# Last stage of a two-layer transformer kernel: the turns of a later pair's routings go behind the last two out_scale products

## The chip, the cores and the metric

The kernel runs on one core of a Trainium2 chip. The metric is the device time of one execution in microseconds (us), from the first to the last instruction with what lies around them. The kernel is one program of four stages that follow each other on the same core; its instructions are written out for each engine by hand, with semaphores between them. Engines are TensorE (PE in the rows), VectorE (DVE), ScalarE (ACT), GpSimd (POOL) and the DMA queue of SyncE (SP).

## The reference

Two layers, each a cross attention and a feed-forward part, on x of 16 batches x 128 positions x 1024. The change lies in the last part, a feed-forward layer with a sign matrix, whose input and output channels are scaled by a softmax routing over 8 experts:

```python
xf = x.reshape(-1, H)                                   # 2048 x 1024, after a layer norm
router_logits = xf @ gate_w.T                           # 8 experts
routing = jax.nn.softmax(router_logits.astype(jnp.float32), axis=1)
in_scale = routing @ in_channel_scale                   # 2048 x 1024
out_scale = routing @ out_channel_scale                 # 2048 x 1024
wb = ste_sign(weight)
out = xf * in_scale @ wb.T * out_scale + bias
x = x + jnp.tanh(g_ffn[1]) * out
```

## The kernel before

The function `sign_ffn_stage` works on pairs of batches; there are 8 pairs, p = 0 to 7, and batch b = 2p or 2p + 1. The loop over p is a software pipeline. In turn p TensorE computes the main products of pair p, the scale products of pair p + 1, and the turns, logits and turned routings of pair p + 2. VectorE also begins the norms of pair p + 3.

The names that the text uses, with the line of each in the profile:

- `main(p, u, part)` (L2411): output u of pair p, batch u // 2 and half u % 2 of the 1024 columns. Each output is two parts of 8 matmuls, 128 rows by 512 columns; the input is split in a rounded piece `xs_hi` and the rest `xs_lo`.
- `turn(b)` (L2362) transposes the normed batch, `logits(b)` (L2370) computes the router's logits, 16 rows by the profile for one batch's call (8 matmuls of 8 columns, two instructions each).
- `route_max`, `route_exp`, `route_share` make the softmax: VectorE's maximum (L2287), ScalarE's exponential (L2214), then on VectorE the reciprocal (L2293), the multiplication (L2296), two copies (L2300) and the rest of the split (L2302). The result is `rt3`, the routing in three pieces of 8, 24 columns in all.
- `turn_routing(b)` (L2378) transposes `rt3` on TensorE; it waits for `rt_hi` and `rt_lo`, which L2300 and L2302 raise. `routing_out(b)` (L2221) copies the result to `rT` on ScalarE.
- `in_scale(p, u)` (L2389) and `out_scale(p, u)` (L2399) multiply `rT` by the 24-row tables. All of them write two PSUM banks in turns, `p_s[0]` and `p_s[1]`. `scale(p, u)` (L2310) applies the in_scale on VectorE, `scale_out(p, u)` (L2226) copies the out_scale to `osc` on ScalarE. `out_scale(p, 2)` waits for `scale_out(p, 0)`, and `out_scale(p, 3)` for `scale_out(p, 1)`, since the bank is the same.
- `finish(p, u)` on VectorE multiplies the main product by `osc` (L2320) and adds it to x (L2323). `add_bias(b)` (L2178) runs on GpSimd, `round_hi` (L2232) on ScalarE and `lo` (L2172) on GpSimd split the scaled input for `main`, `rstd_of` (L2164, L2166) on GpSimd and `norm_apply` (L2280) on VectorE belong to the layer norm.

Each engine runs its own list in the order in which it is written; nothing reorders it, so an instruction that waits holds back all that stand behind it on its engine. VectorE's turn p ends with `finish(p, 2)`, `route_max(2p + 5)`, `route_share(2p + 4)`, `norm_apply(2p + 7)`, `route_share(2p + 5)`. The flags in the code are q (pair p + 1 exists), r (pair p + 2 exists) and z (pair p + 3 exists).

Of the kernel before, what the change touches and what calls it, by code (L numbers as in the profile page):

```python
# [2062 lines left out]
def sign_ffn_stage(nc, banks, x_in, gate, signW, bias, gate_wT, in_scale3, out_scale3, x_out):  # L2063
# [70 lines left out]
    def after(engine, done, count):  # L2134
        if count > 0:
            engine.wait_ge(done, count)

    def cols(b):
        return slice((b % 2) * SEQ, (b % 2 + 1) * SEQ)

    def half(h):
        return slice(h * BANK, (h + 1) * BANK)

    sp, pool, act, dve, pe = nc.sync, nc.gpsimd, nc.scalar, nc.vector, nc.tensor
    def load_x(b):
        sp.dma_start(x_sb[b % RING][:, :], x_in[b]).then_inc(x_land[b % RING], 16)
# [13 lines left out]
    def rstd_of(b):  # L2160
        i = b % 2
        pool.wait_ge(aggregated, b + 1)
        after(pool, xn_done, b - 1)
        G.tensor_tensor(rstd[i][:, :], mv[i][:, 1:2], eps[:, :], ALU.add).then_inc(eps_added, 1)  # L2164
        pool.wait_ge(eps_added, b + 1)
        G.tensor_tensor(rstd[i][:, :], rstd[i][:, :], half_neg[:, :], ALU.pow).then_inc(rstd_done, 1)  # L2166

    def lo(b):
        p = b // 2
        pool.wait_ge(hi_done, b + 1)  # L2170
        after(pool, main_done, 4 * (p - 2) + 4)
        G.tensor_tensor(xs_lo[p % 2][:, :, cols(b)], xs[:, :, cols(b)],  # L2172
                        xs_hi[p % 2][:, :, cols(b)].bitcast(F32), ALU.subtract).then_inc(lo_done, 1)

    def add_bias(b):
        pool.wait_ge(xn_done, b + 1)
        t = x_sb[b % RING][:, :]
        G.tensor_tensor(t, t, tgb[:, :], ALU.add).then_inc(xb_done, 1)  # L2178
# [214 lines left out]
    def out_scale(p, u):  # L2393
        b, h = 2 * p + u // 2, u % 2
        if u < 2:
            pe.wait_ge(xs_done, 4 * p + u + 3)
        else:
            pe.wait_ge(osc_out, 4 * p + u - 1)
        M(p_s[u % 2][:, :], rT[p % 2][:, cols(b)], ocs[:, half(h)], start=True, stop=True)\  # L2399
            .then_inc(out_scaled, 1)  # L2400

    def main(p, u, part):
        b, h = 2 * p + u // 2, u % 2
        if part == 0:
            pe.wait_ge(lo_done, b + 1)
            after(pe, y_done, 4 * p + u - 1)
        for k in range(4 * part, 4 * part + 4):
            if p == 0 and u == 0:
                pe.wait_ge(w_done, k + 1)
            for n, t in enumerate((xs_hi, xs_lo)):  # L2410
                mm = M(p_y[h][:, :], t[p % 2][:, k, cols(b)], w[:, k, half(h)],  # L2411
                       start=(k == 0 and n == 0), stop=(k == KT - 1 and n == 1))
        if part == 1:
            mm.then_inc(main_done, 1)
# [32 lines left out]
    def run():  # L2447
        stack = ExitStack()
        block = stack.enter_context(nc.Block())

        @block.gpsimd
        def _(_):
            for b in range(2, 6):
                rstd_of(b)
            pool.wait_ge(gate_done, 1)
            pool.wait_ge(bias_in, 16)
            G.tensor_scalar(tgb[:, :], tgb[:, :], tg[:, 0:1], None, ALU.mult).then_inc(bias_done, 1)  # L2457
            pool.wait_ge(bias_done, 1)
            add_bias(0)
            add_bias(1)  # L2460

            for p in range(NP):
                for i in range(2):
                    if p + 1 < NP:
                        lo(2 * p + 2 + i)
                    if p + 3 < NP:
                        rstd_of(2 * p + 6 + i)
                if p + 1 < NP:
                    add_bias(2 * p + 2)
                    add_bias(2 * p + 3)  # L2470

        @block.sync
        def _(_):
            load_x(3)
            sp.dma_start(tgb[:, :], bias).then_inc(bias_in, 16)
            for b in range(4, RING):
                load_x(b)
            for b in range(BATCH):
                sp.wait_ge(added, 2 * b + 2)
                sp.dma_start(x_out[b], x_sb[b % RING][:, :]).then_inc(x_store[b % RING], 16)  # L2480
                if b >= 1 and b - 1 + RING < BATCH:
                    sp.wait_ge(x_store[b - 1], 16)
                    load_x(b - 1 + RING)
            for i in range(RING):
                sp.wait_ge(x_store[i], 16 * len(range(i, BATCH, RING)))

        @block.scalar
        def _(_):
            for b in range(2, 4):
                turn_out(b)  # L2490
            for b in range(2, 4):
                route_exp(b)
            for b in range(2, 4):
                routing_out(b)

            for p in range(NP):
                if p + 1 < NP:
                    round_hi(2 * p + 2)
                    round_hi(2 * p + 3)
                if p + 2 < NP:  # L2500
                    turn_out(2 * p + 4)
                    turn_out(2 * p + 5)
                    route_exp(2 * p + 4)
                    route_exp(2 * p + 5)
                if p + 1 < NP:
                    scale_out(p + 1, 0)
                    scale_out(p + 1, 1)
                if p + 2 < NP:
                    routing_out(2 * p + 4)
                    routing_out(2 * p + 5)  # L2510
                if p + 1 < NP:
                    scale_out(p + 1, 2)
                    scale_out(p + 1, 3)

        @block.vector
        def _(_):
            for b in range(2, 4):
                norm(b)
            for b in range(2, 4):
                norm_apply(b)  # L2520
            for b in range(2, 4):
                route_max(b)
            for b in range(2, 4):
                route_share(b)
            for b in range(4, 6):
                norm(b)
            for b in range(4, 6):
                norm_apply(b)

            for p in range(NP):  # L2530
                q, r, z = p + 1 < NP, p + 2 < NP, p + 3 < NP
                if p >= 1:
                    finish(p - 1, 3)
                for u in range(2):
                    if q:
                        scale(p + 1, u)
                finish(p, 0)
                for u in range(2, 4):
                    if q:
                        scale(p + 1, u)  # L2540
                if z:
                    norm(2 * p + 6)
                finish(p, 1)
                if z:
                    norm_apply(2 * p + 6)
                    norm(2 * p + 7)
                if r:
                    route_max(2 * p + 4)
                finish(p, 2)
                if r:  # L2550
                    route_max(2 * p + 5)
                    route_share(2 * p + 4)
                if z:
                    norm_apply(2 * p + 7)
                if r:
                    route_share(2 * p + 5)
            finish(NP - 1, 3)

        @block.tensor
        def _(_):  # L2560
            turn(2)
            turn(3)
            logits(2)
            logits(3)
            turn_routing(2)
            turn_routing(3)

            for p in range(NP):
                q, r = p + 1 < NP, p + 2 < NP
                main(p, 0, 0)  # L2570
                for u in range(2):
                    if q:
                        in_scale(p + 1, u)
                main(p, 0, 1)
                for u in range(2, 4):
                    if q:
                        in_scale(p + 1, u)
                main(p, 1, 0)
                if r:
                    turn(2 * p + 4)  # L2580
                main(p, 1, 1)
                if r:
                    turn(2 * p + 5)
                main(p, 2, 0)
                if r:
                    logits(2 * p + 4)
                main(p, 2, 1)
                if r:
                    logits(2 * p + 5)
                main(p, 3, 0)  # L2590
                for u in range(2):
                    if q:
                        out_scale(p + 1, u)
                main(p, 3, 1)
                if r:
                    turn_routing(2 * p + 4)
                    turn_routing(2 * p + 5)
                for u in range(2, 4):
                    if q:
                        out_scale(p + 1, u)  # L2600

        stack.close()

# [80 lines left out]
```

## Time and profile before

| | |
|---|---|
| median of 3 runs | 3277.77 us (3274.28 to 3280.15) |
| profiled execution, its own time | 3282.62 us |
| profiled execution, span | 3280.8 us |
| mean granted TensorE clock | 0.966 |
| PE busy | 3080.3 us (94%) |
| DVE busy | 1950.1 us (59%) |
| ACT busy | 1229.2 us (37%) |
| POOL busy | 1964.6 us (60%) |

The own time is what the execution took by the device; the span is from its first to its last instruction in the trace. The loop that the change touches takes the last 190 us of the span or so. The granted clock is the share of TensorE's full clock of 2.4 GHz that it was given; 0.5 is 1.2 GHz. A matmul row's duration overlaps its neighbour's, since matmuls are pipelined, so the distance of two starts says more than a duration.

### The profile page before, as it was taken

To read this page: it belongs to the slowest core of one execution; us is meant where nothing else is said; L and a number is where in the kernel's file an instruction comes from. 1 tells how busy PE (TensorE), PEld (TensorE's weight loads), DVE (VectorE), ACT (ScalarE), POOL (GpSimd) and SP (SyncE) were. 2 spreads that over 40 slices of the span, in tenths; PEclk is the share of its full clock that TensorE was granted. 3 is DMA by queue.
4 is the path that set the end of the run, shared out by engine and by line. 5 is a ranking of instruction groups with operands and counts; after the bars stand their busy time and mean duration, and the time that the engine had idled before them with its cause. 6 is when DMAs were issued, how large, how long until landed. Compare 5 with 4: busy or idle time off the path is not lost. (4 is left out here: it accounts for less than half of the span.)

```text
span 3280.8 us, 41110 instructions
## 1 busy us (share of the span) xinstructions
PE 3080.3 (94%) x14547; PEld 2475.3 (75%) x14547; DVE 1950.1 (59%) x2479; ACT 1229.2 (37%) x1898; POOL 1964.6 (60%) x1372
## 2 busy tenths in 40 slices
PE   7999679999999996899999999989999899998799
PEld 6888558788787874677777777777777787777577
DVE  3332257777777753656565666656666566665575
ACT  3111155555555541333333333433333333343222
POOL 4232354454454443777787777777777777775343
PEclk9999889999999997899999999999999999999799
DMA  7343501101111113222233222332222332223211
GB/s 200 107 131 109 181 26 40 65 33 65 52 46 65 43 54 122 89 103 102 89 128 141 102 89 102 121 142 96 101 96 99 118 148 96 108 96 131 84 71 52
DMA packets 171261, 315.54 MB, mean 96 GB/s; under 512 B 10328, under 2 KB 86488, under 8 KB 171144
## 3 DMA queue, kind: packets, MB, share of 16 engines
q1 hardware_dynamic: 171144, 314.04, 27.2%
q8 instruction: 66, 1.08, 0.1%
q14 instruction: 51, 0.42, 0.0%
HBM read 246.90 MB, written 67.11 MB: 96 GB/s over the span
## 5 line engine op out<-in xcount | busy, mean ns | idle before, releaser
L1854 DVE RECIPROCAL g_rsum<-pair 128x512 f32<-128x512 f32 x128 | 429.8, 3358 | 112.9 <-PE pair L1924 109.0
L1892 PE MATMUL pair<-g_xn_hi,g_wq_hi 128*128 128x512 f32 x1024 | 403.6, 394 | 26.9 <-POOL g_wq_lo L1569 22.0
L1892 PE MATMUL pair<-g_xn_lo,g_wq_hi 128*128 128x512 f32 x1024 | 402.0, 393 | 0.0
L1892 PE MATMUL pair<-g_xn_hi,g_wq_lo 128*128 128x512 f32 x1024 | 401.6, 392 | 0.0
L1948 PE MATMUL pair<-g_wo_lo,g_at_hi 128*128 128x512 f32 x992 | 385.9, 389 | 0.0
L1948 PE MATMUL pair<-g_wo_hi,g_at_hi 128*128 128x512 f32 x992 | 385.9, 389 | 0.0
L1948 PE MATMUL pair<-g_wo_hi,g_at_lo 128*128 128x512 f32 x992 | 385.9, 389 | 0.0
L1840 DVE SCALAR_TENSOR_TENSOR g_res<-pair,g_tg,g_res 128x512 f32<-128x512 f32 x256 | 189.8, 748 | 208.9 <-PE pair L1948 207.2
L1569 POOL TENSOR_TENSOR g_wq_lo<-g_wq_raw,g_wq_hi 128x1024 fp32r<-128x1024 f32 x130 | 309.9, 2411 | 1.6 <-ACT g_wq_hi L1720 1.6
L1720 ACT ACTIVATE g_q_hi<-g_q_raw 128x512 fp32r<-128x512 f32 x128 | 81.0, 633 | 575.7 <-POOL g_q_raw L1650 575.7
L669 POOL TENSOR_TENSOR a_qs<-a_qs,a_qrec 128x512 f32<-128x512 f32 x128 | 133.8, 1047 | 202.5 <-DVE a_qrec L915 201.6
L1820 DVE TENSOR_TENSOR g_q_raw<-pair,t_cos_q 128x512 f32<-128x512 f32 x128 | 88.6, 692 | 274.2 <-POOL g_q_raw L1650 148.4
L1650 POOL TENSOR_TENSOR g_q_raw<-g_q_raw,g_rot_b 128x512 f32<-128x512 f32 x128 | 195.5, 1528 | 92.7 <-DVE g_rot_b L1822 92.7
L1892 PEld LDWEIGHTS pair<-g_xn_hi,g_wq_hi 128*128 128x128 f32 x1024 | 194.7, 190 | 71.1 <-POOL g_wq_lo L1569 25.0
L1892 PEld LDWEIGHTS pair<-g_xn_lo,g_wq_hi 128*128 128x128 f32 x1024 | 194.8, 190 | 40.5
L1892 PEld LDWEIGHTS pair<-g_xn_hi,g_wq_lo 128*128 128x128 f32 x1024 | 194.4, 190 | 40.9
L1569 POOL TENSOR_TENSOR g_q_lo<-g_q_raw,g_q_hi 128x512 fp32r<-128x512 f32 x128 | 165.1, 1290 | 95.1 <-ACT g_q_hi L1720 95.1
L1671 POOL TENSOR_TENSOR g_prob_raw<-g_prob_raw,t_keep 128x512 f32<-128x512 f32 x128 | 165.3, 1291 | 85.9 <-ACT g_prob_raw L1751 85.9
L1948 PEld LDWEIGHTS pair<-g_wo_hi,g_at_hi 128*128 128x128 f32 x992 | 186.2, 188 | 39.0
L1948 PEld LDWEIGHTS pair<-g_wo_lo,g_at_hi 128*128 128x128 f32 x992 | 186.2, 188 | 38.8
L1948 PEld LDWEIGHTS pair<-g_wo_hi,g_at_lo 128*128 128x128 f32 x992 | 186.2, 188 | 38.7
L1569 POOL TENSOR_TENSOR g_prob_lo<-g_prob_raw,g_prob_hi 128x512 fp32r<-128x512 f32 x128 | 166.1, 1297 | 47.5 <-ACT g_prob_hi L1720 47.5
(251 smaller groups left out, 7286.1 us busy)
## 6 DMA issues: line engine op xcount, KB each, us to landing
g_wq_raw<-in_L_Wq SPq DMA_DIRECT2D x64, 1024.0 KB, 7.3
g_wo_raw<-in_L_Wo SPq DMA_DIRECT2D x62, 1024.0 KB, 6.2
values_split<-c_v SPq DMA_DIRECT2D x64, 256.0 KB, 2.8
keys_split<-c_k SPq DMA_DIRECT2D x32, 512.0 KB, 2.7
g_k<-keys_split SPq DMA_DIRECT2D x32, 512.0 KB, 3.2
g_v<-values_split SPq DMA_DIRECT2D x32, 512.0 KB, 7.2
c_cx_raw<-in_ctxT SPq DMA_DIRECT2D x16, 512.0 KB, 7.5
a_x<-in_x SPq DMA_DIRECT2D x16, 512.0 KB, 4.4
```

The source lines that it names most:

```text
L669: TT(t, t, spread(qrec[r % 2][:, :], DH), ALU.mult).then_inc(qnorm, 1)
L1569: return engine.tensor_tensor(view(buf["lo"]), view(buf["raw"]), view(buf["hi"]).bitcast(F32), ALU.subtract)
L1650: nc.gpsimd.tensor_tensor(dst, dst, rot_b[:, :], ALU.add).then_inc(rot_done, 1)
L1671: nc.gpsimd.tensor_tensor(heads(e), heads(e), keep[:, :].rearrange("p (o t) -> p o t", o=1) .to_broadcast([P, G, SEQ]), ALU.mult).then_inc ...
L1720: return A(view(buf["hi"]), view(buf["raw"]), ACT.Copy)
L1820: V.tensor_tensor(by_batch(a), by_batch(src[:, :]), w(cos, 0, P), ALU.mult)
L1840: V.scalar_tensor_tensor(out=r, in0=p_y[u % 2][:, :], scalar=tg[:, 0:1], in1=r, op0=ALU.mult, op1=ALU.add).then_inc(y_added, 1)
L1854: V.reciprocal(rsum[:, :], p_sum[:, :]).then_inc(rsum_done, 1)
L1892: mm = M(bank[:, :], w[a][:, i, cols], x[b][:, i, :], start=(i == 0 and t == 0), stop=(i == KT - 1 and t == 2))
L1948: mm = M(p_y[u % 2][:, :], at[p][:, h, bcols(b)], w[r][:, h, half_ * BANK:(half_ + 1) * BANK], start=(h == 0 and t == 0), stop=(h == G - 1 ...
```

## The change

The two turns of the later pair's routings and the last two out_scale products change places at the end of a turn of TensorE's loop. Nothing else is changed: the other engines' lists are the same, and so are all waits.

```diff
@@ -2592,12 +2592,12 @@
                     if q:
                         out_scale(p + 1, u)
                 main(p, 3, 1)
+                for u in range(2, 4):
+                    if q:
+                        out_scale(p + 1, u)
                 if r:
                     turn_routing(2 * p + 4)
                     turn_routing(2 * p + 5)
-                for u in range(2, 4):
-                    if q:
-                        out_scale(p + 1, u)
```

On TensorE, at the end of the loop's turn p = 1 (the difference between before and after; L2411 main, L2399 out_scale, L2378 turn_routing), it looks like this:

```order
 L2411 MATMUL pair<-f_w,f_xs_hi_14045 128x512
 L2411 MATMUL pair<-f_w,f_xs_lo_14046 128x512
+L2399 MATMUL pair<-f_sc_14060,f_rT_14037 128x512 x2
 L2378 MATMUL pair<-f_ident,f_rt_0_14035 24x128
 L2378 MATMUL pair<-f_ident,f_rt_1_14036 24x128
-L2399 MATMUL pair<-f_sc_14060,f_rT_14037 128x512 x2
 L2411 MATMUL pair<-f_w,f_xs_hi_14042 128x512
 L2411 MATMUL pair<-f_w,f_xs_lo_14043 128x512
```

The two products now stand between the last main of pair 1 and the two turns; the first main of pair 2 follows directly behind the second turn. The same holds at six ends, p = 0 to 5.

On ScalarE, the same place, the list is the same before and after (L2232 round_hi, L2207 the turned input, L2214 the exponential, L2226 scale_out, L2221 routing_out):

```order
 L2232 ACTIVATE f_xs_hi_14042<-f_xs 128x8x128 x2
 L2207 ACTIVATE f_xnT_14040<-pair 128x4x128 x4
 L2214 ACTIVATE f_ex_14031,f_small_14029<-pair,f_small_14029 128x8
 L2214 ACTIVATE f_ex_14032,f_small_14030<-pair,f_small_14030 128x8
 L2226 ACTIVATE f_osc_14044<-pair,f_tg 128x512 x2
 L2221 ACTIVATE f_rT_14038<-pair 24x128 x2
 L2226 ACTIVATE f_osc_14044<-pair,f_tg 128x512 x2
```

Nothing moved here: the copies of the turned routings (L2221) stay ahead of the copies of the last two out_scale products.

## Rows read from the trace of the kernel before

**Rows 1.** The page's part 1: busy time by engine.

```profile
PE 3080.3 (94%) x14547; PEld 2475.3 (75%) x14547; DVE 1950.1 (59%) x2479; ACT 1229.2 (37%) x1898; POOL 1964.6 (60%) x1372
```

**Rows 2.** Waits of TensorE in the loop: total, times, longest.

```profile
PE pair L2378 <- DVE f_rt L2302: 4.9, 4, 1.2
PE pair L2362 <- ACT f_xnT L2207: 3.8, 1, 3.8
```

**Rows 3.** The chain that ended last, in the loop: start, us, what.

```profile
3108.54 2.05 PE pair L2411 x8
...
3113.95 2.04 PE pair L2411 x8
...
3133.02 0.27 PE pair L2378
3133.29 0.66 PE pair L2399 x2
3133.95 2.71 PE pair L2411 x8
...
3142.38 2.04 PE pair L2411 x8
...
3162.34 3.61 PE pair L2411 x8
...
3169.31 2.05 PE pair L2411 x8
...
3189.35 3.39 PE pair L2411 x8
...
3196.28 2.05 PE pair L2411 x8
...
3216.27 3.05 PE pair L2411 x8
...
3224.75 2.06 PE pair L2411 x8
```

**Rows 4.** Timeline of turn p = 1: start, us, engine, instruction, [idle before].

```profile
3121.14 0.39 PE L2411 MATMUL pair<-f_w,f_xs_lo 128*128 128x512 f32 x1
...
3123.07 0.49 PE L2411 MATMUL pair<-f_w,f_xs_hi 128*128 128x512 f32 x1
...
3125.21 0.69 DVE L2320 TENSOR_TENSOR f_y<-pair,f_osc 128x512 f32<-128x512 f32 x1 [0.24 <-PE pair L2411]
...
3125.80 5.17 POOL L2178 TENSOR_TENSOR f_x<-f_x,f_tgb 128x1024 f32<-128x1024 f32 x2
...
3128.91 2.10 DVE L2296 TENSOR_SCALAR f_rt<-f_ex,f_small 128x8 f32<-128x8 f32 x1
...
3129.27 1.26 ACT L2226 ACTIVATE f_osc<-pair,f_tg 128x512 f32<-128x512 f32 x2
...
3131.51 0.27 PE L2378 MATMUL pair<-f_ident,f_rt 128*24 128x128 f32 x1
...
3133.02 0.27 PE L2378 MATMUL pair<-f_ident,f_rt 128*24 128x128 f32 x1 [1.23 <-DVE f_rt L2302]
...
3133.75 1.27 ACT L2226 ACTIVATE f_osc<-pair,f_tg 128x512 f32<-128x512 f32 x2 [0.16 <-PE pair L2399]
```

**Rows 5.** Stretches: length, busy us of each engine, granted clock, DMA, GB/s.

```profile
3107.90:3133.00 25.10, 23.87 (x125) 18.51 (x126) 19.71 (x33) 7.91 (x17) 11.63 (x8) 1.00 0.24 85
3135.00:3138.40 3.40, 3.40 (x11) 2.25 (x10) 0.97 (x2) 0.02 (x1) 0.00 (x0) 0.51 0.89 305
3053.10:3056.50 3.40, 3.40 (x10) 2.62 (x9) 0.00 (x0) 3.08 (x4) 0.00 (x0) 0.51 0.00 0
```

**Rows 6.** TensorE's timeline ahead of the loop.

```profile
3050.22 0.72 PE L2399 MATMUL pair<-f_sc,f_rT 24*128 24x512 f32 x2
3051.55 1.07 PE L2399 MATMUL pair<-f_sc,f_rT 24*128 24x512 f32 x2 [0.60 <-ACT f_osc L2226]
3052.55 0.50 PE L1948 MATMUL pair<-g_wq_hi,g_at_hi 128*128 128x512 f32 x1
```

## The prediction

> **What bounds the kernel now.** I read the page first. TensorE is busy 94% of the span [rows 1], so whatever TensorE does not have to wait for is hidden. The change touches only the last stage, and there only the end of a pair's turn in the loop (b is a batch, a pair is two). I therefore asked the trace, in this order: who TensorE waits for in the loop, what the chain of waits looks like around each pair end, what the timeline shows at one such end, and what clock TensorE had.
>
> TensorE waits in the loop in two places only [rows 2]. One is a single 3.8 us at the first pair. The other is the one that the change touches: the turn of the routing (L2378) waits for VectorE's last piece of the split routing (L2302), 4 times, 4.9 us in all. The loop turns routings at six pair ends (p = 0 to 5); at p = 0 and p = 5 the routings are there in time. The four ends with a wait are p = 1 to 4, with the second turn at 3133.02 at p = 1 [rows 3] and 27 to 28 us apart from there on.
>
> The timeline of the end of p = 1 [rows 4] shows the order. The last product of main(1, 3, 1) ends at 3131.50, and the first turn goes at 3131.51, without a wait. The second can't start before 3133.02, since VectorE is late, 1.23 us of idle time. The two scale products (L2399, out_scale(2, 2) and (2, 3)) stand behind it, although nothing that they read or write is missing. Only after them, at 3133.95 by the chain, does the next pair's main begin [rows 3]. So the two products lie on the chain: 0.66 us at each of the four ends.
>
> Why is VectorE late? finish(1, 2) starts at 3125.21, 0.24 us after VectorE came free, so it waits for TensorE and not for its own work; GpSimd's two bias additions run from 3125.80 to 3130.97, and in that time VectorE's 128x8 multiplication (L2296) takes 2.10 us, to 3131.01 [rows 4]. All of that is tied to the in_scale products of the same pair: from their end, where main(p, 1, 0) begins, to the second turn it is 3133.02 - 3113.95 = 19.07 us [rows 3], and the next pairs repeat it. The Trainium skill, page "SBUF — State Buffer", section "SBUF: two separate sides", says that VectorE and GpSimd share a port pair which is locked for a whole instruction; the 2.10 us row agrees. The change moves nothing on either engine, so I leave the 19.07 us as it is.
>
> **The second thing at a pair end: the clock.** After each of these four waits the products slow down. At the end of p = 1 the chain goes from 3133.95 (start of main) to 3142.38 (start of main(2, 1, 0)), which is 8.43 us; the same work after the end without a wait took 3113.95 - 3108.54 = 5.41 us [rows 3]. The granted clock explains it: it is 1.00 (2.4 GHz) over all of 3107.90 to 3133.00, and 0.51, practically the low level of 1.2 GHz, in 3135.00 to 3138.40 [rows 5]. The other three ends give 3169.31 - 3162.34 = 6.97, 3196.28 - 3189.35 = 6.93 and 3224.75 - 3216.27 = 8.48 us [rows 3]. The excess over 5.41 is 3.02, 1.56, 1.52 and 3.07 us, together 9.17 us. This is three and a half times what the two products themselves cost.
>
> **The change, part by part.** No instruction is added or removed. On TensorE two products of 24x512 per pair end go ahead of two turns.
>
> 1. Out of the chain: 2 products, 0.66 us from the chain's row, at the 4 ends with a wait: **2.64 us**. They now run under the wait, from about 3131.50 to 3132.16. The first turn follows (0.27 us, to 3132.43), and the second still starts at 3133.02, since VectorE sets it. The wait left is 0.6 us. At p = 0 and 5 no wait exists, the order of four instructions changes and the sum doesn't: **0**.
>
> 2. A wait moved: out_scale(p + 1, 2) and (p + 1, 3) need ScalarE's copies of the products 0 and 1 out of the same two banks. At p = 1 these run 3129.27 to 3130.53 [rows 4]; TensorE comes at 3131.50. Margin 0.97 us, so **0**. Behind the two products the turns are queued, and behind them ScalarE's copies of the turned routings, the in_scale products and everything else. If the copies were late, all of it would be.
>
> 3. ScalarE's order is as it was: the two turned routings are copied before the scale copies 2 and 3. Before, those two copies ran from 3133.75 to 3135.02. Now their operands lie ready, and they can go behind the second routing copy: it ends some 0.57 us after the turn's start (0.30 to its start and 0.27), so 3133.6, and the pair of 1.27 us ends at 3134.9. The next in_scale products need both; at the full clock they come 2.05 us behind a main that starts at 3133.29, at 3135.3. Margin about 0.4 us for a copy that only the second of them needs: **0**. The other cover, main's own operands, is long there: GpSimd has no work between 3130.97 and the next pair.
>
> 4. The clock: up to **9.17 us**, and this is what has to be decided. The trace has no run of the new order, so I bound it from both sides by what TensorE did before the clock fell. What the four ends have in common is a break between full-size products (128x512 on 128 rows): from 3131.50 to 3133.95 at p = 1 [rows 3, 4], 2.45 us, in which TensorE has two turns, two small products and 1.2 us of nothing. Two earlier breaks of this stage are like it. From 3050.22 to 3052.55, 2.3 us with four 24-row products and 0.60 us idle [rows 6], and the clock was 0.51 in 3053.10 to 3056.50 [rows 5]. On the other side, the logits (16 matmuls of 8 columns) break the full-size products from 3121.14 + 0.39 = 3121.53 to 3123.07 [rows 4], 1.5 us, twice per pair, and the clock stays at 1.00 [rows 5]. With the change the break is 3131.50 to about 3133.25, 1.75 us. So the nearest row is the break of 1.5 us that the clock survived, and 2.3 us is the nearest that it did not. I take the value: no fall, 9.17 us. The lower bound is 0 (all falls stay); a fall that each time lasts as long as the longest one here gives 4 x 3.07 - 9.17 = 3.1 us loss, the bound below zero.
>
> The Trainium skill bears on this on both sides. "TensorE: Matmul & The Clock Gate", section "HAM oscillation — how this bites in real kernels", warns only of long pauses of TensorE; by that rule the clock should not have fallen here at all, with 1.23 us as the longest idle time [rows 4], and the trace contradicts it. The section "A second HAM failure mode: psum-queue depth-cycling" has short idle times between groups of products bring the clock down; by it the 0.6 us that is left could be enough, which is the first rival below.
>
> The sum against the profiled execution's own time, 3282.62 us: 3282.62 - 2.64 - 9.17 = 3270.8 us. That execution is 4.85 us above the median of the three runs (3277.77) and 2.5 above the slowest. How often the clock falls is something a run can differ in (1.5 or 3 us each), so part of the difference is probably a fall more than usual, and what isn't there can't be won. The whole sum off the median gives 3266.0; if all of the 4.85 us were falls, it gives 3270.8. I take the part near the middle: **3269**.
>
> **The rivals.**
> - The clock falls as before (0.6 us idle and two small products are still a disturbance; the break at 3050.22 had just 0.60 us idle). Then only step 1 is won: 3277.77 - 2.6 = 3275.1. For it: that break. Against it: its full-size gap was 2.3 us and had four small products. Chance 0.18.
> - The clock is saved at two of the four ends: 2.64 + 4.6 = 7.2 us off the own time, and 5 or so off the median: 3270 to 3275. Chance 0.12.
> - Nothing is won, as VectorE, given an earlier start, is late by as much again: finish(p, 2) had only 0.24 us of slack [rows 4]. But both it and main(p, 2, 1) are counted from the same in_scale products, so the slack doesn't shrink. 3277.8, chance 0.03.
> - Slower: the exponential of the later pair stands ahead of the scale copies 0 and 1 on ScalarE, and hangs on VectorE. If the copies end after 3131.50, TensorE stands in front of out_scale with both turns queued behind. Up to 3132.2 this costs nothing (3133.02 less 0.27 for a turn and about 0.5 for the products and their start). To be 6.6 us slower in all, with the falls kept, each of the four ends must lose 1.65 us beyond the 0.66 won, so the copies would have to end at about 3134.5, 4 us later than now. Price then 3284.4. Chance 0.04.
>
> **How the numbers follow.** The forecast (no fall at the four ends) has 0.63, its own range 3264 to 3273. A measurement of this kernel tells about 0.2%, 6.6 us, from no change, that is below 3271.2 for faster. The forecast lands there in about nine of ten cases (0.56), the half-saved case in one of three (0.04): faster 0.60. Same: the rest of the forecast 0.07, of the half-saved case 0.08, and the two cases at 3275 and 3278: 0.36. Slower 0.04. The range from 3263.5 to 3276 takes in the first rival and leaves out the last two and the tails.
>
> **What would show it.** In the changed kernel's trace the turns' wait falls from 4.9 to about 2.5 us in 4 places, the L2399 products at p = 1 to 4 directly follow main, and the full-size products resume 0.25 us after the second turn's start. The granted clock is 1.00 from about 3105 to the end, and turn to turn takes 24.8 us (28.39 - 0.66 - 3.02 = 24.7) instead of 26.9 to 28.4 (28.39 is the first period; the others follow from the sizes of their falls). I am wrong if the clock still shows 0.5 behind the second turns, if the second turn comes later than 19.1 us behind the in_scale products, or if TensorE shows a wait for ScalarE's f_osc.

## The result and the profile after

The changed kernel takes 3268.78 us in the median (3265.99 to 3275.14, 8 runs), the kernel before 3278.96 us (3273.85 to 3281.24, 8 runs): a ratio of 0.9973, 95% interval 0.9962 to 0.9984. It is faster by 0.27% by that ratio; the medians lie 10.2 us apart. The forecast was 3269 us.

Busy times by engine, the page's part 1 of the changed kernel (before: [rows 1]):

```profile
span 3267.3 us, 41110 instructions
...
PE 3066.2 (94%) x14547; PEld 2466.3 (75%) x14547; DVE 1948.1 (60%) x2479; ACT 1228.1 (38%) x1898; POOL 1964.4 (60%) x1372
```

The number of instructions is the same, yet TensorE's busy time fell by 14.1 us. Nothing was taken away from it: the same matmuls ran faster. Not all of this is the change's. In the first 3000 us of the span, where both kernels run the same code in the same order, TensorE was busy 2837.5 us in the trace of the kernel before and 2832.2 us in that of the changed one.

TensorE's waits in the loop (before: [rows 2]):

```profile
PE pair L2362 <- ACT f_xnT L2207: 3.8, 1, 3.8
PE pair L2378 <- DVE f_rt L2300: 2.6, 4, 0.7
```

The wait of the second turn is still there four times, at 0.65 us (once 0.69) instead of 1.24. The same place in the timeline, the end of the loop's turn p = 1 (before: [rows 4]):

```profile
3123.91 0.69 DVE L2320 TENSOR_TENSOR f_y<-pair,f_osc 128x512 f32<-128x512 f32 x1 [0.24 <-PE pair L2411]
...
3127.62 2.10 DVE L2296 TENSOR_SCALAR f_rt<-f_ex,f_small 128x8 f32<-128x8 f32 x1
...
3127.97 1.26 ACT L2226 ACTIVATE f_osc<-pair,f_tg 128x512 f32<-128x512 f32 x2
...
3130.13 0.73 PE L2399 MATMUL pair<-f_sc,f_rT 24*128 24x512 f32 x2
...
3130.79 0.28 PE L2378 MATMUL pair<-f_ident,f_rt 128*24 128x128 f32 x1
...
3131.73 0.27 PE L2378 MATMUL pair<-f_ident,f_rt 128*24 128x128 f32 x1 [0.65 <-DVE f_rt L2300]
...
3131.85 0.47 PE L2411 MATMUL pair<-f_w,f_xs_hi 128*128 128x512 f32 x1
...
3132.21 1.23 ACT L2226 ACTIVATE f_osc<-pair,f_tg 128x512 f32<-128x512 f32 x2
```

The products L2399 start at 3130.13 without a wait, 0.90 us after ScalarE's copies ended (3127.97 + 1.26 = 3129.23). Then comes the first turn, then the wait, the second turn at 3131.73, and main at 3131.85. VectorE's 2.10 us row and the 0.24 us in front of finish are what they were.

The chain behind two of the four ends (before: [rows 3]):

```profile
3112.66 2.05 PE pair L2411 x8
...
3131.73 0.27 PE pair L2378
3132.00 1.94 PE pair L2411 x8
...
3137.30 2.05 PE pair L2411 x8
...
3156.37 0.27 PE pair L2378
3156.64 2.08 PE pair L2411 x8
...
3162.09 2.05 PE pair L2411 x8
```

From the start of main(p, 1, 0) to the second turn it is 3131.73 - 3112.66 = 19.07 us, as before. From the start of main behind the second turn to the start of the next main(p, 1, 0) it is 3137.30 - 3132.00 = 5.30 us and 3162.09 - 3156.64 = 5.45 us, where it was 8.43 and 6.97.

Stretches from second turn to second turn, with the granted clock ahead of the two last numbers (before: [rows 5]):

```profile
3107.10:3131.70 24.60, 23.98 (x128) 18.65 (x128) 19.31 (x33) 7.88 (x17) 11.64 (x8) 1.00 0.25 86
3131.70:3156.40 24.70, 24.03 (x127) 18.73 (x127) 19.84 (x33) 7.71 (x16) 11.63 (x8) 1.00 0.25 86
3156.40:3181.20 24.80, 24.15 (x127) 18.69 (x127) 19.78 (x33) 7.71 (x16) 11.62 (x8) 1.00 0.25 87
3181.20:3205.80 24.60, 23.93 (x126) 18.61 (x127) 19.45 (x33) 7.72 (x16) 11.88 (x8) 1.00 0.11 43
3205.80:3229.60 23.80, 23.78 (x126) 18.64 (x127) 13.23 (x25) 7.45 (x15) 9.84 (x4) 1.00 0.11 45
```

The clock is 1.00 throughout. None of the four falls is left.

### The profile page after: what moved, and what is told of

Its sections match the earlier page's. It is cut to its first block and busy times, and to the rows that moved or that the text cites. A ratio compares the mean times of both kernels' runs of the same rounds, so it can differ in the third digit from the quotient of the medians.

```text
span 3267.3 us, 41110 instructions
## 1 busy us (share of the span) xinstructions
PE 3066.2 (94%) x14547; PEld 2466.3 (75%) x14547; DVE 1948.1 (60%) x2479; ACT 1228.1 (38%) x1898; POOL 1964.4 (60%) x1372
```

## The experiments

Two things had to be told apart: product time (the two products leave the chain, 0.66 us at each end) and the clock. And of the clock: what makes it fall, since the forecast took the break between full-size products for it. Each kernel was timed several times, but the two named again, of which there is one execution each. tail_small, tail_full, fill_before and one_product ran on one chip (kernel before 3279.76 us in the median of 24 runs), between_turns, the two share_first and bias_early together (3280.91, 13 runs), and the other four together (3280.39, 21 runs). The changed kernel's own partner took 3278.96 us, so two medians out of different groups can differ by up to 2 us for that alone. The ratios in brackets are each to the kernel before of the same group. Unless said otherwise the extra work of a kernel writes only an idle PSUM bank, and p means p = 1 to 4. A fall is a stretch behind an end in which the granted clock goes to its lower level of 1.2 GHz. The helpers `extra_small` and `extra_full` are not shown; they issue the matmuls that the comments name.

**Time put back, as small or as full products.**

```diff
                     turn_routing(2 * p + 5)
+                if 1 <= p <= 4:
+                    extra_small(p, 2)    # tail_small: rT x ocs, 24 rows, 128x512
+                    extra_full(p, 3)     # tail_full instead: xs_hi x w, 128 rows, 128x512
```

tail_small: 

> The changed kernel with two more 24-row products (128x512, into an idle bank; their result is used by nobody) behind the second turn at p = 1 to 4. It puts back what the change took out of the chain and leaves the order of the real work as changed. Theory (a long break between full-size products makes the clock fall): the break is 2.4 us again, the clock falls behind the second turns, and the time is that of the kernel before, 3279 us, within 4. Rival (only the 0.66 us of product time counts, the clock falls by chance): 2.6 us above the changed kernel, 3271.4.

tail_full: 

> The changed kernel with three more full-size matmuls (128x512 on 128 rows, 0.23 us each, into an idle bank, result unused) behind the second turn at p = 1 to 4. It lengthens the chain by as much as the two small products did, 0.69 us at each end, but the break between full-size products stays 1.75 us. Theory: no fall, 3268.8 + 2.8 = 3271.6 us. Rival (anything that delays the pair brings the falls back): 3279.

tail_small took 3273.64 us (ratio to before 0.9977, 0.9965 to 0.9988), tail_full 3270.53 (0.9972, 0.9961 to 0.9983). By the medians the full-size products cost close to their time and no more: 1.8 us over the changed kernel, 2.8 expected. The small ones cost 4.9 us, 2.6 of it product time. That is not the whole way back to 3279. The two intervals overlap almost wholly, so the times alone don't show that small products cost more than full-size ones. In tail_small's trace one of the four ends has a fall; stretches just behind the ends p = 1 and p = 4:

```profile
3136.40:3139.80 3.40, 3.40 (x16) 2.52 (x16) 1.23 (x3) 0.61 (x2) 0.00 (x0) 1.00 0.71 252
...
3212.30:3215.60 3.30, 3.30 (x9) 2.42 (x8) 0.50 (x1) 0.95 (x2) 0.00 (x0) 0.53 0.39 159
```

So my first theory did not hold as a rule. A break of 2.4 us with 0.65 us of idle time in it went with a fall at one end and with none at three.

**The wait filled, the order left as before.**

```diff
                 if r:
                     turn_routing(2 * p + 4)
+                    if 1 <= p <= 4:
+                        extra_full(p, 4)    # fill_before; small_filled: extra_small(p, 3)
                     turn_routing(2 * p + 5)
```

fill_before: 

> The kernel before, in its order, with four more full-size matmuls between the two turns at p = 1 to 4, under the wait of the second (0.92 us of 1.23; result unused). The real products stay where they were, on the chain. Theory: the break between full-size products ends at 1.1 us, the clock holds, and 9 of the 12 us are won without the change: 3270 to 3272 us. Rival (the order of the products itself does it): no gain, 3279.

small_filled: 

> The kernel before, in its order, with three more 24-row products (about 1 us; result unused) between the two turns at p = 1 to 4, under the wait of the second. The idle time goes from 1.24 to about 0.3 us, the break between full-size products stays 2.45 us. Theory A (the break decides): as the kernel before, 3279 to 3280. Theory B (idle time decides): as fill_before, 3272 to 3273.

fill_before took 3272.86 us (0.9976, 0.9966 to 0.9986). That is 6.9 us under the kernel before of its group: most of the gain comes with no product moved, by work that is thrown away. Its trace has a control in it. At p = 0 nothing was filled, and in this execution that end had a wait too. TensorE's timeline at p = 0, then at p = 1 (L2418 is the filling):

```profile
3103.51 0.27 PE L2378 MATMUL pair<-f_ident,f_rt 128*24 128x128 f32 x1 [1.24 <-DVE f_rt L2302]
...
3128.95 1.17 PE L2418 MATMUL pair<-f_w,f_xs_hi 128*128 128x512 f32 x4
3130.43 0.27 PE L2378 MATMUL pair<-f_ident,f_rt 128*24 128x128 f32 x1 [0.32 <-DVE f_rt L2300]
3130.64 0.73 PE L2399 MATMUL pair<-f_sc,f_rT 24*128 24x512 f32 x2
```

and the stretches behind p = 0, 1, 2, 3 and 4:

```profile
3104.80:3108.10 3.30, 3.30 (x10) 2.23 (x9) 0.00 (x0) 0.70 (x2) 0.00 (x0) 0.53 0.78 263
...
3130.90:3134.30 3.40, 3.40 (x15) 2.28 (x15) 1.18 (x3) 1.38 (x3) 0.00 (x0) 1.00 0.54 181
...
3156.30:3159.70 3.40, 3.40 (x15) 2.27 (x15) 1.22 (x3) 1.37 (x3) 0.00 (x0) 1.00 0.54 177
3181.70:3185.10 3.40, 3.40 (x16) 2.26 (x15) 1.19 (x3) 1.33 (x3) 0.00 (x0) 1.00 0.38 154
3207.00:3210.40 3.40, 3.40 (x15) 2.31 (x15) 1.22 (x3) 1.44 (x3) 0.00 (x0) 1.00 0.38 154
```

The unfilled end falls to 0.53, the four filled ones stay at 1.00.

small_filled took 3276.59 us (0.9992, 0.9983 to 1.0001), 3.8 us under the kernel before of its group by the medians, but the interval does not exclude that nothing was gained. The profiled execution took 3283.20 us, the second slowest of 11. Its trace has all four falls, although the idle time was only 0.33 to 0.35 us. Stretches behind the four ends:

```profile
3135.20:3138.50 3.30, 3.30 (x12) 2.14 (x10) 0.33 (x1) 0.44 (x1) 0.00 (x0) 0.56 0.71 245
3162.50:3165.80 3.30, 3.30 (x9) 2.36 (x9) 0.74 (x2) 1.35 (x3) 0.00 (x0) 0.56 0.51 178
3189.80:3193.10 3.30, 3.30 (x9) 2.24 (x8) 0.44 (x1) 1.18 (x2) 0.00 (x0) 0.56 0.39 159
3217.10:3220.40 3.30, 3.30 (x10) 2.18 (x10) 0.12 (x1) 0.86 (x2) 0.00 (x0) 0.56 0.39 159
```

That speaks against the theory that idle time alone decides: small products in its place did not keep the clock up here, where full-size ones in the same place did.

**More idle time, the order as changed.**

```diff
                     route_share(2 * p + 4)
+                if 1 <= p <= 4:
+                    V.tensor_copy(p_t[0][:, :], tgb[:, 0:BANK])
                 if z:
                     norm_apply(2 * p + 7)
```

idle_more: 

> The changed kernel with one more VectorE copy (128x512, about 0.66 us, result unused) between the shares of the two routings at p = 1 to 4. The second turn comes about 0.66 us later: the chain is as much longer as with the two small products of tail_small, and the break between full-size products is 2.4 us as there, but TensorE is idle in that time (about 1.3 us, not 0.65). tail_small was 4.8 us over the changed kernel. Theory A (my first one, the break between full-size products decides): the same, 3273 to 3274. Theory B (idle time of TensorE decides, small products keep the clock up): the falls of the kernel before come back, 3278 to 3281.

It took 3276.64 us (0.9986, 0.9977 to 0.9995), between the two theories, 3.0 us over tail_small by the medians; the two intervals overlap. The second turn waited 1.21 us, the break was 2.2 us and not 2.4, and three of four ends fell in its trace.

**Half the change.** The edit is against the kernel before.

```diff
                 main(p, 3, 1)
+                if q:
+                    out_scale(p + 1, 2)
                 if r:
                     turn_routing(2 * p + 4)
                     turn_routing(2 * p + 5)
-                for u in range(2, 4):
-                    if q:
-                        out_scale(p + 1, u)
+                if q:
+                    out_scale(p + 1, 3)
```

one_product: 

> Half the change: out_scale 2 ahead of the turns, out_scale 3 behind them. Product time won 4 x 0.33 = 1.3 us. The break between full-size products is 2.1 us, between the 1.75 us that held and the 2.3 to 2.45 us that fell. Theory: some of the four falls stay, 3270 to 3278 us; if break length doesn't matter, 3270.1 (the changed kernel and 1.3).

one_product_again: 

> The kernel with one product ahead of the turns once more, for a second trace. Its first trace shows one fall at the four ends, but its median (3277.4 us) is 7 us above what product time alone gives; if falls make that up, a second trace shows three or four.

It took 3277.37 us (0.9991, 0.9982 to 0.9999; 12 runs, 3272.12 to 3284.13). Half the change brings 2.4 us by the medians, of which product time is 1.3; the whole change brings 10. The first trace (3273.33 us) shows one fall, the second (3281.17 us) three. The stretches of the second behind the four ends:

```profile
3135.00:3138.30 3.30, 3.30 (x11) 2.27 (x9) 0.26 (x2) 0.55 (x1) 0.00 (x0) 0.58 0.73 254
3162.30:3165.60 3.30, 3.30 (x9) 2.35 (x9) 0.90 (x2) 1.38 (x3) 0.00 (x0) 0.58 0.50 168
3189.60:3192.90 3.30, 3.30 (x11) 2.26 (x10) 0.31 (x1) 0.77 (x2) 0.00 (x0) 0.58 0.42 164
3217.40:3220.80 3.40, 3.40 (x15) 2.43 (x15) 1.43 (x4) 1.23 (x3) 0.00 (x0) 1.00 0.38 154
```

One code, 7.8 us apart, with a different number of falls. The loop accounts for 4.5 of the 7.8 us (table below), so falls make up part of the scatter of this kernel's times.

**The kernel before once more.** before_again: 

> The kernel before once more, for a second trace of the same code. If the falls at the four ends are the rule, this one shows at least three of them; if they are a matter of the execution, fewer.

3279.10 us, with a fall behind all four ends, as in the first trace:

```profile
3131.30:3134.70 3.40, 3.40 (x11) 2.29 (x10) 0.63 (x2) 0.30 (x1) 0.00 (x0) 0.54 0.86 295
3158.60:3162.00 3.40, 3.40 (x10) 2.47 (x8) 0.63 (x1) 1.26 (x2) 0.00 (x0) 0.54 0.57 195
3185.90:3189.20 3.30, 3.30 (x9) 2.12 (x9) 0.28 (x1) 1.02 (x2) 0.00 (x0) 0.55 0.39 159
3213.20:3216.60 3.40, 3.40 (x12) 2.37 (x10) 0.00 (x0) 0.65 (x2) 0.00 (x0) 0.55 0.38 154
```

In both traces of the kernel before, the four falls are there; in the one trace of the changed kernel, none is.

**Where the products stand.** Against the kernel before:

```diff
                     turn_routing(2 * p + 4)
-                    turn_routing(2 * p + 5)
                 for u in range(2, 4):
                     if q:
                         out_scale(p + 1, u)
+                if r:
+                    turn_routing(2 * p + 5)
```

between_turns: 

> The two out_scale products between the two turns: turn, product, product, turn. They run under the wait of the second turn as in the changed kernel, but stand behind the first. Theory (what counts is that they are ahead of the turn that waits): as the changed kernel, 3268.8 us within 2. Rival (they must be ahead of both): 3271 or more.

3268.85 us (0.9973, 0.9961 to 0.9984): the changed kernel's time. It is enough that the products stand ahead of the turn that waits.

**VectorE's order.**

```diff
                     route_share(2 * p + 4)
+                    route_share(2 * p + 5)
                 if z:
                     norm_apply(2 * p + 7)
-                if r:
-                    route_share(2 * p + 5)
```

share_first (in the changed kernel): 

> The changed kernel with VectorE's norm_apply(2p + 7) behind route_share(2p + 5) in place of ahead of it. Theory (VectorE alone sets the second turn, in_scale plus 19.07 us): the second turn comes 0.8 us earlier, the wait of 0.65 us that is left is gone, 4 x 0.65 = 2.6 us faster than the changed kernel, 3266.2. Rival (the normed batch is needed at once, or main waits for something else): same as the changed kernel.

share_first_before (in the kernel before): 

> The kernel before, in TensorE's old order, with VectorE's norm_apply(2p + 7) behind route_share(2p + 5). The second turn comes 0.8 us earlier, the products stay behind it. Theory: the break between full-size products is 2.45 - 0.8 = 1.65 us, the clock holds, so 4 x 0.8 + 9.2 = 12.4 us is won without the change, 3266.6 us. If the order of the products matters by itself, only 3.2: 3275.8.

share_first took 3265.40 us (0.9958, 0.9945 to 0.9971), 3.4 less than the changed kernel's median, and is the fastest of all here. The two intervals overlap, and the two kernels weren't timed side by side; the loop in the two traces (table below) shows 3.0 us. In its trace the wait of the turn is gone: the only row of a wait in TensorE's loop is the first pair's.

```profile
PE pair L2362 <- ACT f_xnT L2207: 3.8, 1, 3.8
```

share_first_before took 3270.27 us (0.9967, 0.9955 to 0.9980): 10.6 us under the kernel before, 12.4 expected, with TensorE's old order. Its clock behind the ends p = 1 and 2, then p = 3 and 4, in two long stretches:

```profile
3132.50:3180.00 47.50, 47.01 (x249) 36.77 (x249) 37.80 (x56) 15.29 (x31) 23.20 (x16) 1.00 0.25 89
...
3182.20:3229.80 47.60, 47.11 (x250) 37.06 (x250) 32.21 (x56) 15.03 (x30) 21.49 (x12) 1.00 0.11 45
```

**The bias additions earlier.** On GpSimd, the two `add_bias` calls of a pair were put ahead of its `lo` and `rstd_of` calls.

```diff
             for p in range(NP):
+                if p + 1 < NP:
+                    add_bias(2 * p + 2)
+                    add_bias(2 * p + 3)
                 for i in range(2):
                     ...
-                if p + 1 < NP:
-                    add_bias(2 * p + 2)
-                    add_bias(2 * p + 3)
```

bias_early: 

> The changed kernel with GpSimd's two bias additions of a pair at the head of its turn, ahead of the two subtractions (L2172) and not behind them. Theory (the second turn is late since the bias additions block VectorE's addition, 2.79 us, and multiplication, 2.10 us, behind finish(p, 2)): the wait of the second turn is gone, 2.6 us faster than the changed kernel, 3266.2. Rival: the additions now block VectorE's work on the in_scale products, which main of the next pair hangs on: slower than the changed kernel by 1 us or more per pair.

3270.20 us (0.9969, 0.9958 to 0.9981): nothing gained over the changed kernel. The trace says why. The additions still run at the same place:

```profile
3124.88 0.55 POOL L2166 TENSOR_TENSOR f_rstd<-f_rstd,f_half_neg 128x1 f32<-128x1 f32 x1
3125.40 5.18 POOL L2178 TENSOR_TENSOR f_x<-f_x,f_tgb 128x1024 f32<-128x1024 f32 x2
3125.55 2.79 DVE L2323 TENSOR_TENSOR f_x<-f_y,f_x 128x512 f32<-128x512 f32 x1
```

In a loop the head of turn p + 1 comes right behind the end of turn p, so the additions of the next pair took the place of this pair's. The edit didn't do what it was meant to, and the question of what the additions cost stays open. The trace adds a fall elsewhere: at p = 0 both turns waited (1.40 and 1.23 us), the break was 3.7 us, and the clock was 0.50 behind it.

**The loop alone, in every trace.** The medians carry the scatter of the whole program. The traces allow a closer comparison: the time from the first main behind the end p = 0 to the first main behind the end p = 5, start to start, which spans the four ends.

| kernel | from | to | us | falls at the four ends |
|---|---|---|---|---|
| before | 3108.47 | 3243.11 | 134.6 | 4 |
| before_again | 3105.05 | 3239.60 | 134.6 | 4 |
| changed | 3107.20 | 3229.67 | 122.5 | 0 |
| between_turns | 3104.71 | 3226.99 | 122.3 | 0 |
| share_first_before | 3108.27 | 3230.67 | 122.4 | 0 |
| share_first | 3109.75 | 3229.19 | 119.4 | 0 |
| tail_full | 3103.25 | 3227.90 | 124.7 | 0 |
| tail_small | 3110.77 | 3237.72 | 127.0 | 1 |
| fill_before | 3104.37 | 3231.25 | 126.9 | 0, and one at p = 0 |
| bias_early | 3106.78 | 3230.51 | 123.7 | 0, and one at p = 0 |
| one_product | 3105.98 | 3233.83 | 127.9 | 1 |
| one_product_again | 3109.30 | 3241.67 | 132.4 | 3 |
| idle_more | 3106.47 | 3237.15 | 130.7 | 3 |
| small_filled | 3109.08 | 3243.70 | 134.6 | 4 |

The order of TensorE's products is the old one in share_first_before, and the loop gains the same 12.2 us as with the change: the wait shortened by VectorE's order and the clock kept do as much as the moved products and the clock kept. In small_filled, with the old order and all four falls, it gains nothing.

## Why the prediction was right, point by point

- **What bounds the kernel** held. TensorE waits for VectorE's routing at four ends and nowhere else but at the first pair, and the second turn is 19.07 us behind the in_scale products, to the hundredth. share_first showed the other half: with VectorE's norm of 0.81 us (L2280) moved behind the routing, the wait is gone. In share_first_before, where a wait is left, the second turn comes 18.30 us behind the in_scale products, 0.77 us earlier.
- **Step 1, product time**, 2.64 us. The four ends have the products under the wait. The forecast 0.6 us of wait left was 0.65, and 2.6 us in all instead of the 2.5 forecast.
- **Steps 2 and 3, ScalarE's copies**, cost 0, as forecast. The margin in front of out_scale was 0.90 us (forecast 0.97), no wait for f_osc shows, and the later copies end at 3132.21 + 1.23 = 3133.44, while the in_scale products start 1.94 us behind 3132.00, at 3133.94.
- **Step 4, the clock**, 9.17 us, was taken whole, and no fall came at any of the four ends. The chain from 3112.66 to 3232.42 in the changed kernel (main(1, 1, 0) to main(6, 0, 1)) is 119.76 us, and from 3113.95 to 3245.89 in the kernel before 131.94. The difference is 12.18 us against 11.81 in the sum. That this was the clock, and not the order, is shown by fill_before (filled ends hold, the unfilled one falls) and by share_first_before, both in TensorE's old order.
- **The nearest-row argument for it** was right in outcome and too simple as a rule. I named the break between full-size products. tail_small puts the break at 2.4 us and had one fall in four, small_filled with the same break had four in four. Over all traces of this case no end with a break of up to 1.8 us fell. Of the 29 ends with 2.1 to 2.5 us and no full-size product in the break 21 fell, whether the idle time was 0.33 or 1.24 us, and so did the one with 3.7 us. Length and content of the break don't settle it alone. In one_product's first trace three ends with a break of 2.14 or 2.15 us, 0.88 us of it idle, held and the fourth fell; in the second trace the first three, with 2.14 us, fell and the fourth, with 2.18 us, held. One thing that differs between such ends is the moment at which the break comes. Whether that decides was not tested, and how small products count stays open. The prediction also announces two earlier breaks and gives one (3050.22 to 3052.55). That row is a weak one: in 3046.6 to 3049.5 the granted clock was 0.50 and the full-size products stood 0.43 us apart, so the clock had barely come back before it fell.
- **The median against the own time.** The sum against the own time gave 3270.8, and the profiled execution of the changed kernel took 3269.14. Own time to own time it is 13.5 us, median to median 10.2. Of the 4.85 us of own time over the median I held back about 3 and named a fall more than usual as the likely cause of a part. In the loop there was none more: its falls were the same four in both traces of the kernel before, at 3282.62 and 3279.10 us, and TensorE's busy time in the first 3000 us of the span, 2837.5 and 2833.8 us, differs by 3.7 us, the two times by 3.5. So the difference lies ahead of the loop, and the change could not have lost or won it. Hitting 3269 within 0.3 us is partly luck. The forecast meant a gain of 8.8 us off a median of 3277.77; the gain was 10.2 off a median of 3278.96.

## What to carry to other kernels

When TensorE waits for a short chain on another engine, look at the granted clock behind the wait, not only at the wait: here 4.9 us of waits cost 9 us more in slow matmuls. Put independent matmuls ahead of the instruction that waits, up to the last one whose operands are ready; where none is left, reorder the engine that is waited for, so that the needed result comes first. And judge such an edit by several executions, since the same code fell once in one execution here and three times in another.

## What was unexpected of the hardware

- At the ends of small_filled the clock fell without a wait of TensorE beyond 0.35 us (0.56 granted behind all four). TensorE was busy, with 24-row products and turns. The Trainium skill, "TensorE: Matmul & The Clock Gate", section "HAM oscillation — how this bites in real kernels", speaks of pauses alone; in this trace small products did not do what full-size ones did in fill_before.
- Half an edit can bring less than half: one product ahead of the turns gave 2.4 us by the medians, two gave 10.2.
- A turn directly ahead of main mostly lets main go sooner: at the four ends main's first part takes 1.94, 2.08, 1.92 and 1.94 us on the chain behind a turn, against 2.05 behind a product of 24 rows at the full clock [rows 3]. At the ends without a wait it is 1.84 and 1.85 us. From main's start to the next main(p, 1, 0) the four ends take 5.30, 5.45, 5.29 and 5.31 us, against the 5.41 that the sum used; this is 0.29 of the 0.37 us by which the loop gained more than the sum.
